# Weighing each attention unit in three parts, one bank of sums each, at three different distances behind its score

## The reference, cut to what matters

```python
sim = jnp.einsum('bhid,bjd->bhij', q, k) * SCALE
...
sim = sim + attn_bias
...
sim = jnp.where(causal, neg, sim)
...
attn = jax.nn.softmax(sim, axis=-1)
out = jnp.einsum('bhij,bjd->bhid', attn, v)
```

## Time and profile before

| what | value |
|---|---|
| median of 3 runs | 1587.95 us (1587.29 to 1588.89) |
| the profiled execution | 1586.78 us |
| its span, first to last instruction | 1585.0 us |
| mean granted TensorE clock | 0.972 of full speed |
| batch 0, first score to last low part | 247.9 to 737.3 us |
| batch 1, first low part to last | 978.8 to 1463.1 us |

### The profile page before, as it was taken

The page is one execution under the profiler, slowest core; times in us unless marked ns, Lnnn a source line. Parts: engine busy times, 40 slices in busy tenths (PEclk is TensorE's granted clock), DMA queues, the critical chain, the costliest instruction groups (busy, mean ns, idle before and its releaser), DMA issues.

```text
span 1585.0 us, 39540 instructions
## 1 busy us (share of the span) xinstructions
PE 1439.8 (91%) x13844; PEld 933.9 (59%) x13844; DVE 1201.3 (76%) x2071; ACT 1045.3 (66%) x2140; POOL 1265.3 (80%) x908
## 2 busy tenths in 40 slices
PE   4888986999999999997998995999999999998896
PEld 2444543776776766765443552776776776776342
DVE  4455885788788788784997885788788788787697
ACT  4664654888888888887111554788888888888210
POOL 4564655999999999997563663999999999999553
PEclk9999996999999999998999997999999999999898
DMA  7003963201201111101885885111111111110686
GB/s 210 1 1 81 171 140 80 52 18 41 48 21 41 41 28 41 41 15 28 165 194 140 165 162 106 28 42 41 28 41 41 28 41 41 28 28 1 140 188 151
DMA packets 225620, 114.93 MB, mean 73 GB/s; under 512 B 193200, under 2 KB 193712, under 8 KB 225456
## 3 DMA queue, kind: packets, MB, share of 16 engines
q1 hardware_dynamic: 220864, 104.42, 31.0%
q10 hardware_dynamic: 4608, 8.39, 1.5%
HBM read 58.11 MB, written 8.54 MB: 42 GB/s over the span
## 4 chain that ended last, share of the span: by engine, by line
PE 55%; issue 14%; DVE 11%; POOL 7%; DMA 2%; ACT 2%; DVEq 1%; SPq 1%; ACTq 0%; POOLq 0%
PE ps L1319 16%; PE ps L1283 11%; PE ps L1252 11%; PE ps L1286 11%; DVE work L1055 6%; PE ps L1305 5%; POOL work L587 4%; DVE work L1074 2%; POOL work L604 2%; DMA tab<-bias_table 1%; ACT qo L762 1%; DMA tab<-in_x 1%; PE ps L1189 0%; SPq L449 0%; ACT work L753 0%
## 5 line engine op out<-in xcount | busy, mean ns | idle before, releaser
L574 POOL TENSOR_TENSOR work<-work 128x1024 f16<-128x1024 f32 (+3 forms) x592 | 935.0, 1622 | 53.2 <-ACT work L746 52.6
L1055 DVE SCALAR_TENSOR_TENSOR work<-ps,tab 128x1024 f32<-128x1024 f32 (+3 forms) x640 | 668.9, 1057 | 206.7 <-PE ps L1286 172.5
L746 ACT ACTIVATE work<-work 128x1024 f32<-128x1024 f32 (+3 forms) x640 | 577.3, 923 | 181.3 <-DVE work L1055 175.2
L1319 PEld LDWEIGHTS ps<-vals,work 128*128 128x128 bf16 (+1 forms) x7936 | 429.8, 98 | 112.4 <-POOL work L574 4.2
L1319 PE MATMUL ps<-vals,work 128*128 128x129 f16 (+1 forms) x7936 | 451.2, 207 | 2.8 <-POOL work L574 2.7
L1283 PE MATMUL ps<-qo,kT 128*128 128x512 f16 (+3 forms) x1280 | 345.6, 352 | 52.8 <-DVE work L1055 36.3
L1286 PE MATMUL ps<-qo,kT 128*128 128x512 f16 (+3 forms) x1280 | 344.0, 351 | 0.0
L1286 PEld LDWEIGHTS ps<-qo,kT 128*128 128x128 f16 x1280 | 123.5, 99 | 119.0 <-issue 6.0
L1359 PE MATMUL ps<-wout,work 128*128 128x512 f16 x768 | 175.4, 387 | 15.7 <-DMA work<-work 15.7
L1252 PE MATMUL ps<-wq,tab 128*128 128x512 f16 x768 | 176.4, 380 | 0.5
L1359 PEld LDWEIGHTS ps<-wout,work 128*128 128x128 f16 x768 | 76.4, 100 | 110.1 <-DMA work<-work 15.9
(11 more groups left out here) (135 smaller groups left out, 1300.6 us busy)
## 6 DMA issues: line engine op xcount, KB each, us to landing
tab<-bias_table SPq DMA_DIRECT2D x64, 512.0 KB, 4.6
tab<-in_x SPq DMA_DIRECT2D x64, 256.0 KB, 3.1
out_x<-work ACTq DMA_DIRECT2D x32, 256.0 KB, 2.1
work<-in_L_cond_Wq SPq DMA_DIRECT2D x1, 2048.0 KB, 9.0
work<-in_L_cond_Wout SPq DMA_DIRECT2D x2, 1024.0 KB, 10.4
qo<-in_L_cond_w SPq DMA_DIRECT2D x1, 1024.0 KB, 7.4
work<-work SPq DMA_TRANSPOSE x64, 4.3
qo<-in_L_cond_b SPq DMA_DIRECT2D x2, 256.0 KB, 5.5
```

What stands on the lines that cost most here:

```text
L574: pool.tensor_tensor(low[:, k % LRING, :, c0:512], probs[:, r, :, c0:512], high[:, r, :, c0:512], ALU.subtract).then_inc(low_pool, 1)
L746: act.activation(probs[:, k % RING, :, c0:512], probs[:, k % RING, :, c0:512], ACT.Exp).then_inc(expd, 1)
L1055: dve.scalar_tensor_tensor(out=probs[:, k % RING, :, c0:512], in0=ps[:, 2 * (k % 2):2 * (k % 2) + 2, c0:512], scalar=SCORE, in1=tab[:, :, ...
L1319: last = pe.matmul(ps[:, sum_bank(i, q), (t % SUMS) * VS:(t % SUMS) * VS + w], parts[:, rings[part], e, s * P:(s + 1) * P], vals[:, j, 0:w ...
```

## The change

`LATE` becomes (0, 2, 3): part 0 of a unit is still weighed 6 slots behind its score, part 1 eight slots and part 2 nine slots behind. Within a slot the parts are taken in the order 2, 1, 0. `DRAINS` is built so that each emptying follows its part and no two fall into one slot: block 3's come before the biases of units 20, 23, 25 (before: 20, 21, 23), block 2's 32, 35, 37 (32, 33, 35), block 1's 40, 43, 45 (40, 41, 43), block 0's 46, 47, 49 (44, 45, 47). `STORES` uses the same formula with the new `LATE[2]` and moves from 24, 36, 44, 48 to 26, 38, 46, 50. After the last head pair TensorE has 9 slots without a score instead of 7.

```diff
--- before.py
+++ after.py
@@ -15,6 +15,7 @@
 
 
 
+import itertools
 from contextlib import ExitStack
 
 import concourse.bass as bass
@@ -89,10 +90,12 @@
 
 SUMS = 3
 SUM_TILES = (range(0, 3), range(3, 6), range(6, 8))
-LATE = (0, 0, 1)
+LATE = (0, 2, 3)
 NULLS = {UNITS.index((i, 4 * i + 1)): i for i in BLOCKS}
 
-DRAINS = {UNITS.index((i, 4 * i + 1 + q)) + LAG + LATE[q] + 1: (i, q) for i in BLOCKS for q in range(3)}
+DRAINS = {}
+for i, q in itertools.product(BLOCKS, range(3)):
+    DRAINS[max([UNITS.index((i, 4 * i + 1 + q)) + LAG + LATE[q] + 1] + [slot + 1 for slot in DRAINS])] = (i, q)
 STORES = {UNITS.index((i, 4 * i + 3)) + LAG + LATE[2] + 2: i for i in BLOCKS}
 
 
@@ -1327,13 +1330,12 @@
                         last.then_inc(summed, 1)
 
                 def weigh_slot(hp, s):
-                    for late, qs in ((1, (2,)), (0, (0, 1))):
-                        k = s - LAG - late
-                        for q in qs:
-                            if 0 <= k < NU:
-                                weigh(hp, k, q)
-                            elif k < 0 and hp:
-                                weigh(hp - 1, k + NU, q)
+                    for q in reversed(range(3)):
+                        k = s - LAG - LATE[q]
+                        if 0 <= k < NU:
+                            weigh(hp, k, q)
+                        elif k < 0 and hp:
+                            weigh(hp - 1, k + NU, q)
 
                 def attend():
                     pe.wait_ge(b_cd, NT * (b + 1) + 1)
@@ -1347,7 +1349,7 @@
                         for k in range(NU):
                             score(hp, k)
                             weigh_slot(hp, k)
-                    for k in range(NU, NU + LAG + 1):
+                    for k in range(NU, NU + LAG + LATE[2]):
                         weigh_slot(HP - 1, k)
 
                 def c_project(t, u):
```

## The result

The changed kernel takes 1563.9 us (median of 4 runs, 1560.8 to 1564.89) against 1588.42 before (4 runs): a ratio of 0.9842, 95% interval 0.9825 to 0.9859, so 24.5 us less. The forecast was 1566.2, the range 1562 to 1578. The changed kernel's lines are numbered a little higher: L574 is now L577, L1055 L1058, L1283 L1286, L1319 L1322, L1074 L1077, L762 L765, L794 L797, L587 L590.

What follows compares the result with a forecast made beforehand. TensorE waited for DVE's biases and POOL for ACT's exponentials; POOL would become the bound. Gain 12.0 + 12.0 - 2.2 = 21.8 us, 1586.8 to 1565.0, plus 1.2 for the median: 1566.2 us, range 1562 to 1578.

Steps and rivals of the forecast that it cites:

- What bounds the kernel, before and after: Attention: TensorE waits for DVE's biases, POOL for ACT's exponentials; afterwards POOL's 58.42 us per head pair binds, chance 0.66.
- Step 1 and 2: Weighing later on TensorE, emptyings spread on DVE: bias waits 3.1 to about 1.7 us, their head pair 58.1 us.
- item 2: DVE's emptyings moved: at block 3 to 2, TensorE's waits fall from 0.49 + 0.23 to about 0.13 us.
- Step 3: ACT's store two slots later: POOL's waits of 0.96 us at unit 5 and 0.57 at unit 38 go.
- Step 4 and 5: POOL's wait to reuse its buffer, 1.8 us to spare, and TensorE's waits for free banks: both cost nothing.
- Step 6: End of each batch's attention: block 1's store delays the output stage, costing 1.1 us per batch, 2.2 in all.
- The sum: POOL's idle time in both batches' attention less the tails: 12.0 + 12.0 - 2.2 = 21.8 us gained.
- The rule against it: TensorE's matmul stream at about 81 ns each: full slot 2.16 us, TensorE never waits, gain 0 (1588 us).

Runs made afterwards that it cites:

- the run before: Changed kernel with ACT doing the output stage's first two casts before the last two stores of each batch's attention; 1558.23 us, ratio 0.9799.

## Why the prediction was right

- **What bounds the kernel, before and after.** Right, and shown for POOL: its work can be raised or cut before without effect, and raised after at full price. The head pair came to 58.27 us, forecast 58.4.
- **Step 1 and 2, weighing and emptyings.** TensorE's waits for the bias were to fall from 3.1 to about 1.7 us and fell to 1.1. TensorE's side alone was to take 58.1 us; with POOL relieved it shows 58.02. The count by place holds as well, by the starts of the scores in TensorE's timelines of both kernels: slots 20 to 23 took 6.12 us before and 5.54 after (0.58 less, forecast 0.59), slots 32 to 35 5.21 and 4.47 (0.74, forecast 0.75), slots 40 to 48 13.87 and 13.40 (0.47, forecast 0.4). The wait at slot 22 isn't quite gone, though: slot 21 lasts 1.45 us for 1.30 of work, near the 0.13 that item 2 had left there. What the steps didn't say is which half does it: the run with part 2 later and part 1 not gained nothing, the one with part 1 and 2 at 8 slots gained all. My slot count for that half (58.8 to 59.2 us) was wrong, since the wait of 1.19 us for the bank in slot 46 weighs more than I took it for; a head pair took 59.9.
- **Step 3, the store.** Its effect, no idle time left on POOL at units 5 and 38, came. But I had put POOL's 1.5 us of idle time down to the store's place; the stores alone brought nothing. The idle time goes when TensorE and DVE pass the units on faster, and the store's move is only what the later emptying asks for. The gain was sized by POOL's idle time, and that stays the right measure, as POOL is the next bound.
- **Step 4 and 5, POOL's gate and the banks.** No wait of POOL for TensorE, none of TensorE for a bank, in the changed kernel's attention from 300 us on.
- **Step 6, the tail.** 1.1 us per batch was forecast, 1.24 measured (0.48 to 1.72), by the mechanism named: the store of block 1 was to start 0.45 us before POOL's end and starts 0.33 before it (723.59 against 723.92).
- **The sum.** 24.0 of POOL's waits and 2.2 for the tail gave 21.8; the medians differ by 24.5 (by the interval, 22.4 to 27.8), the profiled executions by 22.5. The traces show two terms that the sum had left out. One is a gain: POOL's busy time in a head pair fell too, from 58.42 to 58.27. When POOL's ops follow closely, each starts about 0.04 us before the end of the one in front (four full ops of 1.896 in 7.47 us), and one behind a wait doesn't; two waits less make 0.08 of the 0.15 us, the other half I can't name. Over 16 head pairs 0.15 us are 2.4 us. The other is a loss of about the same size in the stages that the change doesn't touch (under Open). So in the traces the 21.8 came out nearly right with two missing terms against each other, which is in part luck; the 2 us by which the medians differ more than the traces is no more than the spread of the runs.
- **The rule against it** (81 ns per matmul in a stream, the Trainium skill, "TensorE: Matmul & The Clock Gate", "Back-to-back issue gap"): by it nothing would have been gained. The trace disagrees with that figure, with 44 ns per matmul, and the gain measured bears the trace out.
- **Open.** The profiled execution became shorter by 22.5 us (spans 1585.0 and 1562.5). POOL's stretches from first to last low part shrank by more, and beside the two tails some 2 us came back, spread over the projection and output stages, which the change doesn't touch. The runs of the changed kernel lie 4.1 us apart; I didn't follow this up.

## What to carry to other kernels

Where two engines are both near 97% of a stage, test each by giving it a little more and a little less work: the one whose 1.28 us showed up in full was the bound, whatever the table of waits named. Here a reader of a bank of sums could be moved off the crowded slots with profit only when the next writer of that bank moved as well; moving the emptyings alone cost 1.5%. And when work is made later within a loop, look at the loop's end: here one reordering of ACT's last steps gave back more than the change had lost there.

## What was unexpected of the hardware

The subtraction moved to DVE reads two operands in SBUF. At 569.75 it took 0.77 us, where its neighbours' 192 and 195 columns with one operand in PSUM take 0.35. POOL's op on 384 columns per head was running until 570.24 (568.77 + 1.47), DVE's new op ended 0.28 us after that, and POOL's next one, 512 columns, took 1.22 us instead of 1.05. The same holds for all 32 such ops of the execution: DVE's took between 0.52 and 1.05 us, depending on how much of POOL's op was left, and each ended 0.28 to 0.29 us behind POOL's op; POOL's next one took 1.22 to 1.23 us each time. (A head pair has two of them, so the mean of its five ops on 512 columns is 1112 ns, for 1057 in the run before.) So the two held each other up: DVE's op came to its end only behind POOL's running one, and POOL's next one lost 0.17 us to it. This is the rule of the Trainium skill, "SBUF — State Buffer", section "Who interferes with whom", for a DVE instruction with two SBUF inputs beside a GpSimd instruction that reads SBUF, and this run agrees with it. The price was small because the wait was short and the bias behind it had time: it ended at 571.65 (570.44 + 1.21), and the score two units on, which waits for it, started only at 572.06, by TensorE's timeline. An op of DVE that starts right behind the start of a full one of POOL could, as an estimate from POOL's 1.90 us, wait up to that long, which no run here shows.
